# A token-routed matmul kernel: slot buffers moved onto the first expert's landing area, two landing areas for later weights, y loads from one queue

## The reference

```python
y = depthwise_causal_conv(x, cond_2048[:, None, :]) + b      # 8 taps per channel
logits = einsum('bsh,eh->bse', y, w_router)                   # 8 experts
idx = argmax(logits, axis=-1)
out = x + y @ w_experts[idx].T                                # one 1024x1024 matrix per token
```

## Time and profile before

| | before |
|---|---|
| median of 3 runs | 547.17 us (546.49 to 550.29) |
| profiled execution | 548.22 us |
| its span | 546.3 us |
| mean granted TensorE clock | 0.972 |
| busy: TensorE, VectorE, ScalarE, GpSimd | 508.5, 284.5, 149.1, 132.1 us |
| HBM read and written | 94.56 and 35.45 MB |

### The profile page before, as it was taken

One profiled execution on the slowest core, in us unless ns is written; L12 is line 12 of the kernel. 1 busy time (PEld: TensorE's weight loads), 2 busy tenths in 40 slices (PEclk: granted clock), 3 DMA queues, 4 the chain that ended last, 5 costly groups with the idle time before them and its releaser, 6 DMA issues.

```text
span 546.3 us, 9011 instructions
## 1 busy us (share of the span) xinstructions
PE 508.5 (93%) x2740; PEld 439.2 (80%) x2741; DVE 284.5 (52%) x369; ACT 149.1 (27%) x255; POOL 132.1 (24%) x148
## 2 busy tenths in 40 slices
PE   5999999696299999999699999999999999999995
PEld 5999999696288787888488888888888888888884
DVE  5854473345765523429748432277227722475581
ACT  2443434254200101115525100061006100151430
POOL 1004132060243013321122131210322032121323
PEclk9999999799599999999799999999999999999998
DMA  8958979996646895668999765459646965579635
GB/s 314 401 155 260 352 228 365 245 316 263 176 195 232 273 308 149 188 197 298 314 283 364 244 174 172 122 201 360 187 130 192 347 179 165 155 241 295 192 120 187
DMA packets 59187, 130.28 MB, mean 238 GB/s; under 512 B 12704, under 2 KB 32416, under 8 KB 59168
## 3 DMA queue, kind: packets, MB, share of 16 engines
q1 hardware_dynamic: 19392, 58.22, 32.6%
q0 software_dynamic: 14832, 54.27, 28.2%
q10 hardware_dynamic: 24944, 17.55, 13.4%
HBM read 94.56 MB, written 35.45 MB: 238 GB/s over the span
## 4 chain that ended last, share of the span: by engine, by line
PE 59%; issue 3%; DMA 2%; DVE 1%; ACTq 1%; ACT 0%; POOL 0%; DVEq 0%; POOLq 0%
PE ps L747 59%; DMA x_row<-x_rows,idx 2%; DVE w_sb L591 1%; ACT w_sb L377 0%; ACTq L271 0%; DVE x_row L613 0%; DMA out<-x_row,idx 0%; ACTq L393 0%; DVE ys L605 0%; DVE y_cols L600 0%; POOL out L815 0%; DVEq L616 0%; ACTq L391 0%; ACTq L273 0%; ACTq L380 0%
## 5 line engine op out<-in xcount | busy, mean ns | idle before, releaser
L747 PE MATMUL ps<-w_sb,ys 128*128 128x512 f32 x1680 | 386.7, 393 | 19.7 <-issue 13.1
L747 PEld LDWEIGHTS ps<-w_sb,ys 128*128 128x128 f32 x1680 | 318.2, 190 | 87.5 <-issue 15.5
L705 PE MATMUL ps<-mats,xs 128*128 128x128 f32 x1024 | 121.2, 283 | 7.6 <-DMA xs<-x_both 5.8
L705 PEld LDWEIGHTS ps<-mats,xs 128*128 128x128 f32 x1024 | 119.9, 199 | 7.8 <-DVE mats L440 5.4
L600 DVE STREAM_TRANSPOSE y_cols<-y_blk 128x1024 f32<-128x1024 f32 x36 | 44.8, 1244 | 146.5 <-PE ps L747 121.1
L386 ACT CAST ys<-y_cols 128x1024 fp32r<-128x1024 f32 x36 | 37.9, 1053 | 276.4 <-DVE y_cols L600 260.4
L591 DVE TENSOR_TENSOR w_sb<-w_raw,w_sb 128x1024 fp32r<-128x1024 f32 x64 | 73.9, 1219 | 26.5 <-ACT w_sb L377 26.4
L377 ACT CAST w_sb<-w_raw 128x1024 fp32r<-128x1024 f32 x64 | 62.2, 1045 | 28.3 <-issue 16.9
L815 POOL DMA_INDIRECT out<-x_row,idx x35 | 40.8, 1164 | 94.9 <-DVE x_row L613 90.1
L803 POOL DMA_INDIRECT y_sorted<-rows,pos_i x32 | 35.0, 1093 | 102.2 <-PE ps L705 64.1
L822 POOL COPY idx<-ids_all 128x1 int32 (+1 forms) x36 | 12.0, 335 | 178.9 <-DMA out<-x_row,idx 139.1
(11 more groups left out here) (88 smaller groups left out, 33.9 us busy)
## 6 DMA issues: line engine op xcount, KB each, us to landing
w_raw<-experts SPq DMA_DIRECT2D x64, 512.0 KB, 7.6
y_blk<-y_sorted ACTq DMA_DIRECT2D x132, 128.0 KB, 3.7
xs<-x_t SPq DMA_DIRECT2D x48, 256.0 KB, 5.9
xs<-x_both SPq DMA_DIRECT2D x16, 512.0 KB, 7.9
y_blk<-y_sorted SPq DMA_DIRECT2D x20, 128.0 KB, 2.7
x_row<-x_rows,idx POOLq DMA_INDIRECT x36, 4.7
out<-x_row,idx POOLq DMA_INDIRECT x35, 4.8
ids_all<-y_sorted ACTq DMA_DIRECT2D x33, 1.0 KB, 4.5
```

The costliest lines, as they stand in the source:

```text
L705: mm = nc.tensor.matmul(to, xs[:, n % X_RING, s % PACK, :], mats[:, s, :].rearrange("p (u n) -> p u n", n=SIDE), start=(s == sets[0]), sto ...
L747: mm = nc.tensor.matmul(out_ps[k][:, f * HALF:(f + 1) * HALF], ys[k][:, a, c, :], w_sb[:, c, b, f * HALF:(f + 1) * HALF], start=(c == 0 an ...
```

## The change

1. The start: the first pack's `x` and factors are loaded in two parts, the first matrices built in two halves, and the constants' load waits for the first pack's `x`.
2. Routing: `choose` comes two `double`s earlier.
3. The slot buffers lie over the leading expert's landing area (now `w_first`), chunk by chunk: `y_blk` over chunks 0 and 1, `y_cols` over 2 and 3, `ys0` over 4 and 5, `x_row` over 6 and 7. The y loads of slots 0 and 1 go out in the midst of the `x` loads (after packs 60 and 62) and wait for `w_split`.
4. Later weights land in two areas over `rows[0]` and `rows[1]`, used in turn; the table's third row says which (`sign`). The second and third expert's 16 chunks are issued one after the other with no wait between.
5. All y loads are issued by SyncE.
6. The table's row numbers are converted first, with a semaphore of their own (`rows_ready`).

```diff
+Y_AFTER = [(LAST + 1) * PACKS - 4, (LAST + 1) * PACKS - 2]
-FACTOR_PACKS = [(0, 2), (2, 8), (8, PACKS)]
+FACTOR_PACKS = [(0, 1), (1, 2), (2, 8), (8, PACKS)]
+START_SETS = PACK // 2
...
-        y_blk = over("y_blk", [P, RING, 4, HC, PIECE], rows_at)
-        y_cols = [over(f"y_cols{k}", [P, HC, P], rows_at + (8 + 4 * k) * KB) for k in range(RING)]
-        x_row = over("x_row", [P, RING, H], rows_at + 16 * KB)
+        w_raw = [over(f"w_raw{k}", [P, HC, H], rows_at + k * row_bytes) for k in range(2)]
+        y_blk = over("y_blk", [P, RING, 4, HC, PIECE], raw_at)
+        y_cols = [over(f"y_cols{k}", [P, HC, P], raw_at + (8 + 4 * k) * KB) for k in range(RING)]
+        x_row = over("x_row", [P, RING, H], raw_at + 24 * KB)
...
+                if n in Y_AFTER:
+                    t = Y_AFTER.index(n)
+                    sp.wait_ge(y_out[t], TPG * 16)
+                    sp.wait_ge(w_split, t + 1)
+                    load_y(sp, lead_row(t), t, ids_all[:, t:t + 1, :])
-            sp.wait_ge(y_out[0], 2 * TPG * 16)
-            sp.wait_ge(y_out[1], TPG * 16)
-            for t in range(RING):
-                load_y(sp, lead_row(t), t, ids_all[:, t:t + 1, :])
...
-            with sp.Fori(0, EXPERTS - 1) as n:
-                with sp.If(n < loads):
...
-                        sp.wait_ge(w_split, n * HC + (c + 1))
-                        load_raw(e, c)
+            for k in range(2):
+                with sp.If(k < loads):
+                    e = sp.value_load(load_i[0:1, k:k + 1], min_val=0, max_val=EXPERTS - 1)
+                    for c in range(HC):
+                        sp.dma_start(w_raw[k][:, c, :], chunk(e, c)).then_inc(raw_in[k][c], 16)
+            sp.wait_ge(y_blocks, FIRST + 1)
+            load_slot(FIRST + 2, (FIRST + 2) % RING)
+            replace_raw(FIRST, loads)
...
+                        sp.wait_ge(y_blocks, t + 2)
+                        load_slot(t + 3, (FIRST + k + 1) % RING)
+                        replace_raw(t + 1, loads)
...
                 if b == BANKS - 1:
+                    act.wait_ge(w_split, 6)
                     high_y(0, 0)
...
             act.wait_ge(table_ready, 1)
-            load_slot(FIRST + 2, (FIRST + 2) % RING)
             high_w(FIRST)
...
                         high_y(t + 1, (FIRST + k + 1) % RING)
-                        load_slot(t + 3, (FIRST + k + 1) % RING)
                         high_w(t + 1)
...
+                step(V.tensor_scalar(sign, flag, -2.0, 1.0, ALU.mult, ALU.add))
+                step(V.tensor_tensor_scan(sign, sign, const(C_ZERO), 1.0, ALU.mult, ALU.add))
+                step(V.tensor_scalar(sign, sign, 0.5, 1.5, ALU.mult, ALU.add))
+                step(V.tensor_tensor(sign, sign, flag, ALU.mult))
...
-                for k in range(5):
+                for k in range(3):
                     double(n + k)
                 choose(g - 1)
-                double(n + 5)
-                double(n + 6)
+                for k in range(3, 7):
+                    double(n + k)
                 place_rows(g - 1)
...
-            low(0, 4)
+            low(0, 4, w_first)
+            dve.wait_ge(w_split, 3)
             turn_blocks(0, 0, 1)
-            low(0, 5)
+            low(0, 5, w_first)
+            dve.wait_ge(w_split, 4)
             turn_blocks(1, 1, 1)
...
-            pool.wait_ge(y_out[0], 2 * TPG * 16)
+            pool.wait_ge(w_split, HC)
             for t in range(RING):
                 look_up(t, t, 1, t + 1)
                 gather_x(t, idx[:, t:t + 1])
```

More of the change, by code:

```diff
@@ L248, in build @@
         third_known = sem("third_known")
+        rows_ready = sem("rows_ready")
         table_ready = sem("table_ready")
-        raw_in = [sem(f"raw_in{c}") for c in range(HC)]
+        first_in = [sem(f"first_in{c}") for c in range(HC)]
+        raw_in = [[sem(f"raw_in{k}_{c}") for c in range(HC)] for k in range(2)]
         w_hi = sem("w_hi")
@@ new lines, in _ @@
+            sp.wait_ge(y_blocks, FIRST + 1)
+            load_slot(FIRST + 2, (FIRST + 2) % RING)
+            replace_raw(FIRST, loads)
+            last = sp.value_load(one_i[0:1, 3:4], min_val=0, max_val=ROUNDS - 1)
+            with sp.Fori(0, ROUNDS) as i:
+                with sp.If(i < last + 1):
+                    for k in range(RING):
+                        t = i * RING + (FIRST + k)
+                        sp.wait_ge(y_blocks, t + 2)
+                        load_slot(t + 3, (FIRST + k + 1) % RING)
+                        replace_raw(t + 1, loads)
@@ L372, in evict, with high @@
                 nc.scalar.copy(to, conv_bank(n)[:, 0:m * SIDE].rearrange("p (c j i) -> p j c i", j=PHASES, i=CH)).then_inc(conv_out, 1)
[L374 to L380, removed]
-                load_y(act, row, k, ids_all[:, bass.ds(t, 1), :])
+            def high(c, raw, arrived, count):
+                act.wait_ge(arrived, count)
+                nc.scalar.copy(w_sb[:, c, HI, :], raw[:, c, :]).then_inc(w_hi, 1)
             def high_y(t, k):
@@ L389, in high_w @@
             def high_w(t):
-                new = act.value_load(tab_i[0:1, 2, bass.ds(t, 1)], min_val=0, max_val=1)
-                with act.If(new == 1):
-                    nth = act.value_load(tab_i[0:1, 1, bass.ds(t, 1)], min_val=1, max_val=EXPERTS - 1)
-                    for c in range(HC):
-                        act.wait_ge(gemm_chunk, (t - 1) * HC + (c + 1))
-                        high(nth, c)
+                new = act.value_load(tab_i[0:1, 2, bass.ds(t, 1)], min_val=0, max_val=2)
+                for k in range(2):
+                    with act.If(new == k + 1):
+                        nth = act.value_load(tab_i[0:1, 1, bass.ds(t, 1)], min_val=1, max_val=EXPERTS - 1)
+                        for c in range(HC):
+                            act.wait_ge(gemm_chunk, (t - 1) * HC + (c + 1))
+                            high(c, w_raw[k], raw_in[k][c], nth * 8 + 8 * (1 - k))
             for g in range(LAST):
@@ L409, in _ @@
                     act.wait_ge(conv_mm, sets_done(LAST, 2 * PACK * (ready[0] + 1)))
-                    high(0, ready.pop(0))
+                    c = ready.pop(0)
+                    high(c, w_first, first_in[c], 16)
             high_y(1, 1)
@@ L498, in place_rows @@
                 step(V.tensor_copy(base, place[:, TPG, :]))
-            count, lead, others, rest, start, n_of, flag, more, nth, tmp, tail, done = (per[:, i, :] for i in range(1, 13))
+            count, lead, others, rest, start, n_of, flag, more, nth, tmp, tail, done, sign = (per[:, i, :] for i in range(1, 14))
             full_row = one[:, 5:6]
@@ L567, in slot_table @@
                 step(V.tensor_scalar(tab[:, 0, :], tab[:, 0, :], full_row, None, ALU.add))
+                V.tensor_copy(tab_i[:, 0, :], tab[:, 0, :]).then_inc(rows_ready, 1)
                 step(V.tensor_tensor(val, inside, per_slot(nth), ALU.mult))
                 step(V.tensor_reduce(tab[:, 1, :], val, AX.X, ALU.add))
-                step(V.scalar_tensor_tensor(out=val, in0=late, scalar=0.0, in1=per_slot(flag), op0=ALU.is_equal, op1=ALU.mult))
+                step(V.scalar_tensor_tensor(out=val, in0=late, scalar=0.0, in1=per_slot(sign), op0=ALU.is_equal, op1=ALU.mult))
                 step(V.tensor_reduce(tab[:, 2, :], val, AX.X, ALU.add))
-                step(V.tensor_copy(tab_i[:, :, :], tab[:, :, :]))
+                step(V.tensor_copy(tab_i[:, 1:3, :], tab[:, 1:3, :]))
                 into = cmp[:, 0, 0:EXPERTS, :]
@@ L615, in low_w @@
             def low_w(t):
-                new = dve.value_load(tab_i[0:1, 2, bass.ds(t, 1)], min_val=0, max_val=1)
-                with dve.If(new == 1):
-                    nth_load = dve.value_load(tab_i[0:1, 1, bass.ds(t, 1)], min_val=1, max_val=EXPERTS - 1)
-                    for c in range(HC):
-                        low(nth_load, c)
+                new = dve.value_load(tab_i[0:1, 2, bass.ds(t, 1)], min_val=0, max_val=2)
+                for k in range(2):
+                    with dve.If(new == k + 1):
+                        nth_load = dve.value_load(tab_i[0:1, 1, bass.ds(t, 1)], min_val=1, max_val=EXPERTS - 1)
+                        for c in range(HC):
+                            low(nth_load, c, w_raw[k])
             for n in range(PACKS):
@@ L645, in _ @@
                     for c in range(4):
-                        low(0, c)
+                        low(0, c, w_first)
                         double(n + 8 + 2 * c)
@@ L697, in conv @@
                         pe.wait_ge(doubled, n - PACKS + 1)
+                if g == 0 and s == START_SETS:
+                    pe.wait_ge(mats_ready, 2)
+                    pe.wait_ge(x_in[0], 16)
                 sets = bank_sets(b)
```

82 lines of the change are left out of this document (53 added, 29 removed).

## The result

The changed kernel takes 553.03 us in the median of 8 runs (551.27 to 554.92), the kernel before 547.80 in its 8: a ratio of 1.0102, with a 95% interval of 1.0078 to 1.0126. It is slower by about 1%, in the range and on the side forecast, 2 us under the forecast. Two terms of the sum were mis-sized, in opposite directions, and part of the nearness is luck: the profiled execution of the changed kernel is the fastest of its 8, and against it the forecast of 556.0 us is 4.7 us too high.

A forecast was written before the change was run, and what follows sets the result against it. TensorE, busy 93% of the span, was taken as the bound, so only its waits could pay. From 548.2 us, -0.7 + 0 + 8.0 + 2.5 - 2.0 = +7.8 gave 556.0, forecast 555 us for the median, range 543 to 564.

The forecast's parts named there:

- The start: Before the first matmul: halved operations and fewer bytes ahead gain 0.7 us, bounds 0 and 1.5.
- it carries through: At the start: the 0.7 us gain is kept, as everything up to group 3 moves with TensorE.
- The first slot: Before slot 0: y loads delay pack 63 to 137.0, slot starts at 146.0, nothing gained beyond the start's 0.7 us.
- `choose` at nothing: Rank matmuls of group 2: the 4.30 us wait goes but moves into small pack waits; gain 0, bounds 0 and 4.3.
- Slot 5: Ahead of slot 5: its y load waits behind 16 weight chunks on SyncE's queue; loss 8.0 us, bounds 4.7 and 13.8.
- the stream's length: Ahead of slot 5: weights, one scatter and one gather take 20.8 + 2.6 us from 181.6, ending at 205.0.
- The clock behind it: After the gap at slot 5: matmuls run at the low clock for a while, adding 2.5 us.
- Slot 10: Ahead of slot 10: without ScalarE's y issues the 5.16 us gap shrinks, gain 2.0 us, bounds 0 and 4.5.
- without the issues about 2.4 us go: Ahead of slot 10: taking the y load's five issues off ScalarE saves about 2.4 us before `high`.
- The second branch: Ahead of slot 10: a branch on ScalarE for the two landing areas costs some 0.3 to 0.4 us.
- the 7 to 10 named: Sign of being right: a gap of 7 to 10 us ahead of slot 5, behind the y load's DMA.
- the gap of about 3 us ahead of slot 10: Sign of being right: about 3 us of the gap ahead of slot 10 remains.

The follow-up runs named there:

- e4: The changed kernel with the y loads of slots 0 and 1 behind all x loads: 549.02 us, ratio 1.0043 to the kernel before.
- e3: The changed kernel with SyncE's order altered to slot 5's y, 8 weight chunks, slot 6's y, 8 chunks: 540.58 us, ratio 0.9900 to the kernel before.
- e2: The kernel before with the y loads of slots 5 and later issued by SyncE, single landing area kept: 538.67 us, ratio 0.9871 to the kernel before.
- e8: The changed kernel with the old start, first pack and factors whole, constants first: 552.55 us, ratio 1.0107 to the kernel before.
- e7: The changed kernel with `choose` behind five doubles again: 550.99 us, ratio 1.0086 to the kernel before.
- e1: The changed kernel with the y loads of slots 5 and later issued by ScalarE again: 546.85 us, ratio 1.0014 to the kernel before.
- e9: The changed kernel with first y loads behind all x, slot 5's y before the weights, third expert's chunks behind slot 7's y: 533.24 us, 0.9755 to the kernel before.

## Why the prediction was right, and where it was not

**The start: -0.7 predicted, nothing measurable found.** The step that failed is "it carries through". Group 0's rank was at 42.34 before and is at 42.41 now: the 1.83 us went into waits for the next packs, which a faster start doesn't bring sooner. With the new start group 0's rank came between 41.54 (e4) and 42.86 (e3), with the old one at 42.34, 42.66 (e2) and 42.80 (e8), and e8's time is the changed kernel's.

**The first slot: right, by its own steps.** Predicted were pack 63 at 137.0 and the slot at 146.0; measured were 137.32 and 146.07, the slot 8.75 us behind the pack. The counts bear the mechanism out: 955 packets of GpSimd's queue against 952 of SyncE's from 118 to 130, one for one, and then, as the scatter runs out, 751 of SyncE's in 4 us. e4 shows the cost directly. It takes one more thing away that the prediction left out: SyncE stood 9.8 us at the wait for the first chunk of `w_split` ahead of slot 0's y, so pack 61's load was issued at 117.86 (e4: 106.14). SyncE's queue had work all that time (share 102% of 16 engines from 105 to 110 and 103% from 110 to 115), so this speaks for the packets, but no run has the wait without the y loads. `choose` at nothing was right (e7).

**Slot 3: 0.5 us not foreseen.** It starts 35.84 us after slot 0, against 36.33 before. The first 18 matmuls took 5.92 us instead of 6.43, and the granted clock in the first 3 us (third from the end) was 0.70 instead of 0.50, after a wait of 3.20 us instead of 13.09. Before and changed:

```profile
146.60:149.60 3.00, 2.94 (x7) 2.41 (x8) 2.76 (x9) 0.00 (x0) 0.00 (x0) 0.50 0.38 125
...
146.00:149.00 3.00, 2.93 (x9) 2.39 (x10) 2.76 (x9) 0.23 (x1) 0.00 (x0) 0.70 0.00 0
```

**Slot 5: the mechanism right, the size 10.6 where 8.0 stood.** The stream began earlier than I had it, at 176.99 instead of 180.70. Before, SyncE waited for the whole table ahead of slot 3's y and issued it at 173.48; now it goes out at 169.99. So that load had not only waited for group 3's scatter, as I had written, and I had cost the change at nothing. It should have helped by 3.7 us. But the term that failed is the stream's length: I gave it 23.4 us from its first packets (9.44 MB at 403 GB/s) and its end at 205.0, and the last of the 16 chunks landed at about 208.4, 20.5 us after its issue. The rate in 40 slices of 203 to 209, SyncE's queue there, and that last chunk's issue (187.9 to 189.4):

```profile
GB/s 328 464 410 382 328 396 362 294 232 109 246 102 198 150 143 164 116 130 164 205 205 247 145 185 199 192 164 212 198 273 225 198 205 212 198 273 205 253 255 213
...
q1 hardware_dynamic: 1327, 1.34, 109.6%
...
w_raw<-experts SPq DMA_DIRECT2D x1, 512.0 KB, 20.5
```

The bulk is through after the eighth slice, at 204.2, where the rate falls from some 400 GB/s to 200 and SyncE's queue has mostly y pieces left; up to there 10.03 MB went by at a mean of 383 GB/s from 178. A few weight packets follow until 208 (22 packets of over 2 KB from 204.2 to 208), and the last chunk is complete only with them. The transpose comes at 211.24, 2.8 us behind that, less than my 4.0. The four pieces and the row numbers of a slot count on one semaphore, so the trace doesn't tell which of them came last. SyncE was done with issuing slot 5's y at 198.68, long before the last weights landed: it is the queue that held the load and not the issuing.

Of the 10.6 us, 1.1 are no loss of the stream: TensorE came to slot 5 that much sooner, and waited. The size also differs between executions (12.63 in e7's, 14.83 in e8's). e1 and e3 each take the whole gap away.

**The clock behind it: 2.5 predicted, 1.8 measured.** Busy time in stretches of the changed kernel, PE first and the granted clock third from the end:

```profile
212.00:215.00 3.00, 0.00 (x0) 0.00 (x0) 2.82 (x3) 1.04 (x1) 0.57 (x1) 0.50 0.25 64
215.00:218.00 3.00, 2.95 (x7) 2.38 (x8) 2.45 (x3) 1.04 (x1) 0.71 (x1) 0.50 0.87 288
218.00:221.00 3.00, 3.00 (x12) 2.43 (x12) 1.13 (x1) 0.00 (x0) 1.15 (x2) 0.86 0.36 97
```

The clock is at its lower level, 1.2 GHz (0.50), at the end of the wait and in the first 3 us of the matmuls, and mostly back in the next 3 (0.86). 1440 matmuls took 328.47 us; at the 226.9 ns that e9 has (1344 in 304.92) they take 326.7.

**Slot 10: -2.0 predicted, -7.7 measured; this term was mis-sized.** Its step was "without the issues about 2.4 us go". I took ScalarE's y issues at slot 10 alone. ScalarE of the changed kernel in order of time, which answers to the earlier trace rows:

```profile
252.55 3.90 ACT L420 CAST w_sb<-w_raw 128x1024 fp32r<-128x1024 f32 x4 [0.42 <-PE ps L808]
...
264.18 1.05 ACT L425 CAST ys<-y_cols 128x1024 fp32r<-128x1024 f32 x1 [2.45 <-DVE y_cols L646]
...
265.82 7.70 ACT L420 CAST w_sb<-w_raw 128x1024 fp32r<-128x1024 f32 x8 [0.58 <-issue]
```

At slot 9, too, `high` now follows 0.42 us behind its release. Before, that row of ScalarE was

```profile
244.98 7.71 ACT L377 CAST w_sb<-w_raw 128x1024 fp32r<-128x1024 f32 x8 [4.19 <-issue]
```

with 4.19 us of its own issuing ahead of it. So now VectorE's remainders end sooner and slot 10's transpose is no longer late. And at slot 10 the 4.36 us of the earlier trace rows become 0.58: the table reads that I counted as staying cost almost nothing without DMA issues ahead of them. My reading is that they now run while `high_y` still does, as the first y issue did before (it began at 257.21, `high_y` ended at 257.48). The second branch that I had at 0.3 to 0.4 us is at most 0.16: e2, with one area, has 0.42 where 0.58 stands here. The gap of 5.16 us goes whole, and with it the low clock, 274.75 - 1200 x 0.2269 = 2.5 us. e1 and e2 show that ScalarE's issuing made the gap and the landing area had no part in it.

Together: -0.6 (slot 0) - 0.5 (slot 3) + 10.6 + 1.8 (slot 5) - 7.7 (slot 10) = +3.6, against 3.1 between the spans; slots 5 to 9 before were 0.2 us above 226.9 ns a matmul, and the end behind the last matmul is 0.3 us shorter now. The forecast's 7.8 was too high because slot 10 gives back nearly four times what I had allowed, beyond its bound of 4.5, while slot 5 takes more. The two errors, 5.7 us one way and 2.6 the other, cancel in part. And the medians are 5.2 us apart where the profiled executions are 3.1: the median execution of the changed kernel is 1.8 us above the profiled one. The longer gaps ahead of slot 5 in e7 and e8 point to where that lies; no trace of a median execution shows it. So a forecast only 2 us off owes something to both. Of its signs, the 11.09 us ahead of slot 5 lie outside the 7 to 10 named, and the gap of about 3 us ahead of slot 10 did not come.

The Trainium skill's rule of "DMA: Bandwidth & Descriptors", section "Issuing engines are not separate DMA queues", that issuing from several engines only saves the sequencer's issue time, doesn't hold here if it is read to mean that the issuer makes no other difference: with the issuer alone changed, e1 is at 1.0014 where the changed kernel is at 1.0102, in the direction that a queue's own order gives. The issue time of the rule is what slot 10 shows.

## What to carry to other kernels

A DMA that the next step waits for must not be queued behind a bulk load that is needed much later; the order within a queue decided 2% here, with the same bytes by the same queue. Before loads are moved to another engine, list what stands ahead of them there, and what the old engine does right behind them: the issues taken off ScalarE were worth 7.7 us. An earlier start of a stage that waits for DMAs gave nothing measurable here, and neither did loading the third expert's weights long before their use. A profile is one execution: where the wait that matters ends with a DMA, its length can differ by some us between executions of the same order (11.09, 12.63 and 14.83 us).

## What the runs showed that I had not expected

With 16 weight DMAs outstanding, SyncE needed 6.29 us to issue the four pieces of slot 5's y (row 190.15 above), against 1.85 us for four otherwise; e8 has 6.27 us at the same place. In these runs a queue with much in it holds the issuing engine as well.

The end of a bulk load is not where the rate falls: at slot 5 the rate fell at 204.2, and the last chunk was complete at 208.4.
